# Selective-scan tower: decay slots that go round over the groups, and the unread matmuls left out

## The reference

```python
def _ssm_layer(x, A_log, Dp, W_dbc, W_dt, b_dt):
    A = -jnp.exp(A_log)
    dbc = jnp.einsum('ble,ce->blc', x, W_dbc)
    delta, Bm, Cm = jnp.split(dbc, [DT_RANK, DT_RANK + N_STATE], axis=-1)
    delta = jax.nn.softplus(jnp.einsum('blr,er->ble', delta, W_dt) + b_dt)
    dA = jnp.exp(delta[..., None] * A)
    dBx = (delta * x)[..., None] * Bm[:, :, None, :]
    # h[t] = dA[t] * h[t-1] + dBx[t], for 64 channels x 64 states
    y = jnp.einsum('blen,bln->ble', hs, Cm)
    return y + Dp * x
```

## Time and profile before

| | us |
|---|---|
| median of 3 runs | 6378.29 (6377.5 to 6378.56) |
| the profiled execution | 6375.66 |
| its span, first to last instruction | 6373.7 |
| first scan to end of last scan | 40.4 to 5966.7, 5926.3 |
| scans (L905), busy | 5770.1 |
| `u` times B (L1102), busy | 5786.8 |
| mean granted TensorE clock, share of 2.4 GHz | 0.911 |

### The profile page before, as it was taken

The page is one execution under the profiler, slowest core; times in us unless marked ns, Lnnn a source line. Parts: engine busy times, 40 slices in busy tenths (PEclk is TensorE's granted clock), DMA queues, the critical chain, the costliest instruction groups (busy, mean ns, idle before and its releaser), DMA issues.

```text
span 6373.7 us, 115806 instructions
## 1 busy us (share of the span) xinstructions
PE 5068.4 (80%) x35437; PEld 2072.7 (33%) x35437; DVE 5961.3 (94%) x4016; ACT 4973.1 (78%) x10250; POOL 5855.3 (92%) x964
## 2 busy tenths in 40 slices
PE   6777777878787878787877777777777777777799
PEld 2333333333333333333333333333333333333354
DVE  7999999999999999999999999999999999999733
ACT  6888888888888888888888888888888888888433
POOL 7999999999999999999999999999999999999411
PEclk8899999898989898989899999999989999999899
DMA  7888778888888888888888888888888888887300
GB/s 239 262 262 261 261 261 262 259 264 259 262 260 262 260 264 259 262 260 263 259 263 263 264 262 258 261 263 261 262 259 263 262 265 263 265 263 265 120 8 10
DMA packets 561477, 1561.79 MB, mean 245 GB/s; under 512 B 172113, under 2 KB 320338, under 8 KB 561170
## 3 DMA queue, kind: packets, MB, share of 16 engines
q1 hardware_dynamic: 561298, 1559.93, 76.0%
HBM read 1469.00 MB, written 90.59 MB: 245 GB/s over the span
## 4 chain that ended last, share of the span: by engine, by line
DVE 44%; issue 24%; PE 16%; POOL 10%; ACT 2%; DMA 2%; DVEq 1%; SPq 0%; ACTq 0%; POOLq 0%
DVE hT L905 43%; POOL u L1102 10%; PE z_bank L412 4%; PE decay L394 4%; PE decay L533 3%; ACT decay L686 2%; PE prep_bank L533 2%; DMA u<-dx_rows 1%; PE z_bank L422 1%; PE z_bank L533 1%; PE prep_bank L493 1%; DVEq L904 1%; PE prep_bank L438 1%; DVE dx L916 1%; ACT z_sb L695 0%
## 5 line engine op out<-in xcount | busy, mean ns | idle before, releaser
L1102 POOL TENSOR_TENSOR u<-u,Bt 128x2976 f32<-128x2976 f32 x896 | 5786.8, 6493 | 166.3 <-DMA u<-dx_rows 164.2
L905 DVE TENSOR_TENSOR_SCAN hT<-decay,u 128x744 f32<-128x744 f32 x3584 | 5770.1, 1684 | 134.5 <-ACT decay L686 111.0
L686 ACT ACTIVATE decay<-decay,a_neg 128x371 f32<-128x371 f32 (+2 forms) x7168 | 3633.5, 555 | 627.6 <-PE decay L394 600.1
L394 PE MATMUL decay<-stk,spread 96*128 96x371 bf16 (+2 forms) x7168 | 1911.9, 355 | 1258.0 <-DVE hT L905 1159.6
L412 PE MATMUL z_bank<-hT,Cst 128*32 128x256 f32 x21504 | 1620.2, 424 | 6.6 <-DVE hT L905 4.3
L394 PEld LDWEIGHTS decay<-stk,spread 96*128 96x128 bf16 x7168 | 448.9, 100 | 2814.0 <-DVE hT L905 2606.6
L695 ACT COPY z_sb<-z_bank 128x512 f32<-128x512 f32 x1344 | 805.9, 600 | 384.9 <-PE z_bank L412 384.0
L412 PEld LDWEIGHTS z_bank<-hT,Cst 128*32 128x32 f32 x21504 | 598.2, 117 | 787.0 <-issue 533.2
L422 PE MATMUL z_bank<-stk,spread 96*128 96x372 bf16 x1341 | 330.1, 361 | 0.0
L493 PEld LDWEIGHTS prep_bank<-tmap,yT 64*128 64x128 f32 x1344 | 207.0, 219 | 134.4 <-issue 134.4
L493 PE MATMUL prep_bank<-tmap,yT 64*128 64x32 f32 (+3 forms) x1344 | 246.6, 308 | 0.0
(11 more groups left out here) (132 smaller groups left out, 2519.2 us busy)
## 6 DMA issues: line engine op xcount, KB each, us to landing
u<-dx_rows SPq DMA_DIRECT2D x3584, 372.0 KB, 4.1
delta_parts<-parts SPq DMA_DIRECT2D x112, 279.0 KB, 6.9
stk<-delta_parts SPq DMA_DIRECT2D x112, 279.0 KB, 5.1
y_rows<-z_sb SPq DMA_DIRECT2D x1792, 12.0 KB
yT<-y_rows SPq DMA_DIRECT2D x112, 192.0 KB, 4.7
dx_rows<-dx SPq DMA_DIRECT2D x112, 186.0 KB, 2.7
xT<-in_x SPq DMA_DIRECT2D x64, 186.0 KB, 4.3
xP<-in_x SPq DMA_DIRECT2D x64, 186.0 KB, 3.9
```

The costliest lines, as they stand in the source:

```text
L394: nc.tensor.matmul(slot[:, e, :, 1:], spread[0:PARTS * QR, TILES_G * q + er // TILES_G, :], src[:, er % TILES_G, :, 1:], start=True, stop= ...
L686: last = nc.scalar.activation(bank, bank, ACT.Exp, scale=a_neg[:, l, c:c + 1])
L905: nc.vector.tensor_tensor_scan(hT[q % 2][:, i * PAIR:(i + 1) * PAIR], pair_slot(p), u[c % RING][:, part * PAIR:(part + 1) * PAIR], 0.0, AL ...
L1102: tt(here, here, Bt[buf][:, :].unsqueeze(1).broadcast_to([P, 2 * HALVES * CHUNK, W0]), ALU.mult).then_inc(s_u, 1)
```

## The change

Three things are changed.

1. Slots: a group gets a `turn`, PAIRS times the number of the groups before it, modulo 3, and place p uses slot (turn + p) % 3. With that each place of each group but the first waits for the scan three places earlier, also across the border of two groups.
2. Loops: the turn must be known when the code is built, and it repeats every three groups; buffers repeat every two. So the hardware loop's body holds six groups instead of two (`ROUND_OF_GROUPS = 6`). Before it stand 2, 6 and 2 groups in the three layers, after it 2, and the loop runs 10, 4 and 2 times (before: 30, 14 and 6).
3. `keep_busy` and its calls are taken out, with their waits.

```diff
+ROUND_OF_GROUPS = 6
-        def pair_slot(p):
-            return db[p % SLOTS][:, BANK - W0:BANK + W0]
+        def pair_slot(turn, p):
+            return db[(turn + p) % SLOTS][:, BANK - W0:BANK + W0]
+            def turn(l, g):
+                return PAIRS * (gbase[l] + g) % SLOTS
             for l in range(LAYERS):
                 n = groups[l]
-                for g in range(2):
-                    body(g % 2, *group(l, g))
-                with eng.Fori(1, n // 2 - 1) as k:
-                    for half in range(2):
-                        body(half, *group(l, 2 * k + half))
+                first = 2 + (n - 4) % ROUND_OF_GROUPS
+                for g in range(first):
+                    body(g % 2, turn(l, g), *group(l, g))
+                with eng.Fori(0, (n - 2 - first) // ROUND_OF_GROUPS) as k:
+                    for g in range(ROUND_OF_GROUPS):
+                        body(g % 2, turn(l, first + g), *group(l, ROUND_OF_GROUPS * k + (first + g)))
                 for g in range(n - 2, n):
-                    body(g % 2, *group(l, g))
+                    body(g % 2, turn(l, g), *group(l, g))
-                if p >= SLOTS:
+                if p >= SLOTS or not known_below(n, 1):
                     pe.wait_ge(s_scan, PAIRS * n + p - SLOTS + 1)
-                elif not known_below(n, 1):
-                    pe.wait_ge(s_scan, PAIRS * n - (2, 1, 3)[p] + 1)
-            def keep_busy(at, buf, q):
-                if q or not known_below(G(at), 1):
-                    pe.wait_ge(s_zev, FILLS * (TILES_G * G(at) + q))
-                for _ in range(3):
-                    nc.tensor.matmul(zb[:, 0:W0], spread[0:PARTS * QR, 0, :], stk[buf][0:PARTS * QR, 0, :],
-                                     start=True, stop=True)
-                    if p in (8, 16, 24) or p == 1 and prev:
-                        keep_busy(here, half, -1 if p == 1 else q - 1)
```

More of the change, by code:

```diff
@@ L315, in store_h, with body @@
                 sp.dma_start(hs[l][:, bass.ds(g * n, n)], y_out[:, 0:n]).then_inc(s_store, 16)
-            def body(half, here, prev, before, after):
+            def body(half, turn, here, prev, before, after):
                 for c in range(CHUNKS):
@@ L377, in _, with spread_delta @@
             pe.wait_ge(s_neg, 2)
-            def spread_delta(at, buf, p):
+            def spread_delta(at, buf, turn, p):
                 l, _ = at
@@ L384, in spread_delta @@
                     pe.wait_ge(s_stk, 16 * (n + 1))
-                if p >= SLOTS:
+                if p >= SLOTS or not known_below(n, 1):
                     pe.wait_ge(s_scan, PAIRS * n + p - SLOTS + 1)
-                elif not known_below(n, 1):
-                    pe.wait_ge(s_scan, PAIRS * n - (2, 1, 3)[p] + 1)
                 q, i = divmod(p, TPAIRS)
-                slot = pair_slot(p).rearrange("p (e s t) -> p e s t", e=2, t=T)
+                slot = pair_slot(turn, p).rearrange("p (e s t) -> p e s t", e=2, t=T)
                 src = stk[buf][0:PARTS * QR, :, :].rearrange("p r (s t) -> p r s t", t=T)
@@ L496, in to_channels, with body @@
                     last.then_inc(s_Y, 1)
-            def body(half, here, prev, before, after):
+            def body(half, turn, here, prev, before, after):
                 for p in range(PAIRS):
-                    spread_delta(here, half, p)
+                    spread_delta(here, half, turn, p)
                     q, i = divmod(p, TPAIRS)
@@ L670, in _, with decay @@
             act.wait_ge(s_zero, 5)
-            def decay(at, p):
+            def decay(at, turn, p):
                 l, g = at
                 T = LENGTHS[l]
-                slot = pair_slot(p)
+                slot = pair_slot(turn, p)
                 act.wait_ge(s_arg, D * G(at) + 2 * p + 1)
@@ L766, in post, with body @@
                 nc.scalar.copy(y_out[:, 0:w], prep[:, 0:w]).then_inc(s_post, 1)
-            def body(half, here, prev, before, after):
+            def body(half, turn, here, prev, before, after):
                 for p in range(PAIRS):
-                    decay(here, p)
+                    decay(here, turn, p)
                     q, i = divmod(p, TPAIRS)
@@ L894, in _, with scan @@
             dve.wait_ge(s_cast, 1)
-            def scan(at, p):
+            def scan(at, turn, p):
                 n = G(at)
@@ L904, in scan @@
                 dve.wait_ge(s_dec, PAIRS * n + p + 1)
-                nc.vector.tensor_tensor_scan(hT[q % 2][:, i * PAIR:(i + 1) * PAIR], pair_slot(p),
+                nc.vector.tensor_tensor_scan(hT[q % 2][:, i * PAIR:(i + 1) * PAIR], pair_slot(turn, p),
                                              u[c % RING][:, part * PAIR:(part + 1) * PAIR], 0.0,
@@ L916, in times_x, with body @@
                 tt(dx[:, :], prep[:, 0:W0], xT[buf][:, :], ALU.mult).then_inc(s_dx, 1)
-            def body(half, here, prev, before, after):
+            def body(half, turn, here, prev, before, after):
                 for p in range(PAIRS):
-                    scan(here, p)
+                    scan(here, turn, p)
                     if after and p == 9:
```

## The result

The changed kernel takes 6399.88 us (median; 6392.65 to 6403.31) against 6378.29 us before: a ratio of 1.0031 with a 95% interval of 1.0022 to 1.0039, so it is slower by 0.31%, some 21.6 us. The forecast was 6375, a gain of 0.05%: the time lies within the range, but the sum put its centre 25 us too low, and what was forecast as no change is a small loss, clear of the interval. The profiled execution took 6392.65 us, 17.0 more than the 6375.66 of the one before.

A forecast was written before the change was run, and what follows sets the result against it. VectorE's pace was taken as the bound, with some 145 us of stalls. From the profiled 6375.7 us, - 88.8 (slots) + 62 (matmuls) + 23 (loop body) = 6372, as median 6375 us; own range 6335 to 6415, overall 6300 to 6460.

The forecast's parts named there:

- What bounds the kernel: Scan part: VectorE sets the pace, least 51.6 us a group; some 145 us are its stalls, ending with ScalarE's decay.
- The slots: Group borders: with slots going round, the stalls ahead of places 0 to 3 go, 88.8 us gained.
- The unread matmuls: Places 29 to 31: without them the clock falls in nearly every group, late stalls 112 us instead of 49.9, 62 lost.
- The longer body: Jumps back of the loop: code must be loaded again, 13 x 1.8 = 23 us lost, ends 0 and 51 us.
- code at its upper bound: Rival at the 13 jumps back: code loading costs its upper end, 6403 us; chance 0.08.
- The clock needs no help: Rival at place 24: clock falls stay as frequent as now, late stalls stay at 49.9, 6313 us; chance 0.28.
- Early in every group: Rival: clock low from place 25 on always, every group pays 1.8 us, 6465 us; chance 0.18.
- The low clock outlasts the border: Rival at places 5 to 9: low clock costs some 3 us in every second group, 6540 us; chance 0.06.
- Theory A: Posed before the experiments: slots bring about 89 us, matmuls cost about 57, 13 jumps at about 4 us cost 54.
- theory C: Rival posed before the experiments: the terms are not independent; what one part takes away, another gives back elsewhere.

The follow-up runs named there:

- fixed_kb_r6: The kernel before with loop bodies of six groups alone, slots fixed and unread matmuls kept: 6417.94 us.
- rot_kb: The changed kernel with `keep_busy` and its calls put back (unread matmuls at places 1, 8, 16 and 24): 6373.25 us.
- nokb_only: The kernel before without `keep_busy`, slots fixed and loop bodies of two groups: 6403.38 us.
- rot_kb24_r30: The changed kernel with loop bodies of thirty groups (one jump back) and three unread matmuls put back at place 24 alone: 6316.84 us.
- rot_kb2_r120: The changed kernel with all groups written out and unread matmuls put back at places 1, 8, 16 and 24, six instead of three at 24: 6259.26 us.
- rot_kb24x3_r120: The changed kernel with all groups written out and nine unread matmuls at place 24 alone: 6230.79 us.
- rot_kb2_r30: The changed kernel with loop bodies of thirty groups and unread matmuls back at places 1, 8, 16 and 24, six instead of three at 24: 6250.26 us.

## Why the prediction was right or wrong

**What bounds the kernel: right.** VectorE's stalls made up the difference in all kernels, nearly all of them behind ScalarE's decay. A scan part of 5780.0 us, 51.6 us a group, was reached when they were gone. GpSimd, idle for 166.3 us in the kernel before, is without a gap there too; no scan but the first waits for it even then.

**The slots: right by place.** All of the gaps ahead of places 1 to 3 went, except behind a jump and at the start, and TensorE's gap at the border is 1.11 us, where about 1.1 was foretold. Not all of the 88.8 us was the slots' to begin with: 8.3 us stood at place 0 behind the 18 jumps of the two later layers, where ScalarE waits for code. By edit they were worth half of the 88.8 us. `fixed_kb_r6` to `rot_kb`, the step that changes nothing but the slots, is 44.7 us: the early stalls fell by 83.4 us, from 142.6 to 59.2, near the term, but the late ones rose from 33.2 to 72.1, which the sum had at nothing.

**The unread matmuls: right in size, in part by luck.** 112 us of late stalls were forecast and 107.0 came, with the two patterns of the earlier trace rows as their form. The size was put together as nearly 112 groups at 1.0 us. It is 78 groups at 1.37 us, and the two errors cancel: that is luck. As a level it holds better than as a step: without the matmuls late stalls are 107.0, 119.1 and 114.0 us, whatever slots and loops do. But the forecast gave the whole rise from 49.9 to the missing matmuls. One chain of kernels, each one edit from the next, divides it:

```
                     median us   step    late stalls   early stalls
before                 6378.29                 49.9         92.2
fixed_kb_r6 (loops)    6417.94   +39.7         33.2        142.6
rot_kb      (slots)    6373.25   -44.7         72.1         59.2
after       (matmuls)  6399.88   +26.6        107.0         54.2
```

The stalls account for the steps. From kernel to kernel their sum changes by +33.7, -44.5 and +29.9 us, and the profiled executions, in which they were counted, by +33.5, -46.1 and +29.6.

The loops took 17 us of late stalls away, the slots brought 39 back, the matmuls 35. With the slots fixed and the short loops the same matmuls were worth 69 (`nokb_only`), so each share holds for its own neighbours only. The reason that I gave for the clock (places 23 to 26 sit on the edge, and 0.63 us of unread matmuls at place 24 carry them over it) is borne out by `rot_kb24_r30` and by the series three, six, nine at place 24: 76.0, 18.1, 0 us. (The first of these has one jump, the others none, which six matmuls have shown to be worth some 20 us of luck.) The others, at places 1, 8 and 16, did no good that can be told with the slots going round. That those at place 1 did harm while the slots were fixed is the reading of `nokb_only`.

**The longer body: the step that failed.** The sum had 13 x 1.8 = 23 us, with an end at 51. In the changed kernel's trace it is 46.7 us at place 0 and 3.7 at place 1, 50.5 us at the 13 jumps. By itself, in two kernels that differ in nothing else, it is 53.1 us. That is 27 to 30 us more than the sum had, and the whole miss of 25 us; the late stalls came 5 us lower, and the median stood 7.2 us above the profiled execution and not 2.6. The term was right in its kind and in the number of jumps, and even the rival "code at its upper bound" (6403 us) stands near the result. What was mis-sized is the load. It was taken as 3 to 4 us, from ScalarE's rows in the second layer, where ScalarE alone had to load. For that case the 1.8 us are borne out: the 13 jumps of the second layer cost 2.0 us each in `nokb_only`. When the loop's body is three times as long, TensorE's, VectorE's and SyncE's code is gone as well, and each of the loads is longer: 5.2 to 6.6 us from the branch on TensorE, up to 6.3 on VectorE and 5.8 on ScalarE. VectorE was given 1.6 us of lead against 3 to 4 us; its own load ends last at 6 of the 13 jumps. That the 50.5 us stay just within the end of 13 x 3.95 is luck, since that end was the same row of the same engine, and single gaps reach 4.73 us. The lead of 1.75 us that was set against it was nearly right: 6.14 less the 1.11 that TensorE idles anyway, less 3.50 that reached VectorE, leaves 1.5.

The section "ISA Cache" of the page "Advanced Engine Details and Errata" of the Trainium skill, by which neither TensorE's nor ScalarE's body of six groups would be held, agrees with the 6.31 and 4.51 us from their branches at the first jump.

**The rivals.** "The clock needs no help" fell: late stalls stayed nowhere at 49.9 without the matmuls (107.0, 119.1 and 114.0). "Early in every group" would have asked for 202 us of late stalls; 107 came, since 41 groups of 112 have no stall at place 29. "The low clock outlasts the border" is not seen: in the changed kernel no place from 4 to 9 has a stall of over 0.1 us, and in `nokb_only` two have, 0.17 and 0.28 us. Theory A holds for the jumps, theory C for the other two parts.

**What stays open.** Why the falls come where they do. The granted clock and the busy time of a stretch don't say it: 13.20 us of 13.3 busy at 0.51 (above). Why the slots raise the late stalls, and why one kernel has 3 such falls in one execution and another, which differs by a jump, 13 (`rot_kb2_r120`), was not worked out.

## What to carry to other kernels

Cost a jump back by the code that every engine must load at once, and take its price from a row of that engine, not of another: here about 2 us of the critical path for each jump when ScalarE alone had to load and nothing hid it, about 4 us once the bodies of TensorE and VectorE are too long as well, and nothing for code written out in order. Where several small stalls have a cause in common (here a clock that falls), do not add up what each removal gains; an edit that removes one may move the fall to another, and two edits together can be worth more than their sum, as 5 us (six matmuls at place 24) and 67 us (slots and long loops) apart became 128 together. And when extra work is put in to hold the clock, find the one place where it acts and put enough there: nine matmuls at one place did what twelve at four places did not.

## What the hardware showed that I had not expected

**The price of a jump.** At the first jump of the changed kernel TensorE's idle time is 6.14 us and ScalarE's 5.69; ScalarE alone had 2.68 to 3.22 in the kernel before. VectorE, whose code was held before, waits for it up to 6.3 us from its branch. The packets of the instruction queues rose by 259 on q8 (from 49) and by 235 on q14 (from 130). Their number alone isn't a cost: all written out (`rot_kb24x3_r120`) there are 274 and 182, and the scan part has no gap that would be a load. Only the load behind a jump is waited for.

**A low mean clock is not a cost in itself.** The window of the scan part for `rot_kb2_r30` and for the faster `rot_kb24x3_r120`:

```profile
40.40:5834.00 5793.60, 4447.28 (x34487) 1813.26 (x34487) 5779.03 (x3695) 4859.48 (x9958) 5775.26 (x895) 0.97 0.83 268
```

```profile
42.70:5822.70 5780.00, 4456.02 (x33818) 1794.79 (x33818) 5777.43 (x3695) 4829.34 (x9958) 5773.45 (x895) 0.93 0.83 268
```

The clock is 0.97 in the one and 0.93 in the other, and the second is 13.6 us shorter. Its low stretches are mostly at the borders (80 of 111 have a mean clock below 0.75), where nothing waits for TensorE once the slots go round. A window at such a border has a granted clock of 0.50 and VectorE busy throughout:

```profile
1130.00:1135.00 5.00, 5.00 (x38) 1.45 (x31) 5.00 (x4) 3.40 (x8) 5.00 (x2) 0.50 0.90 258
```

The place of the fall decides, not the share of the time at 1.2 GHz.
